# Where the feed-forward weights are split into halves: at each later stage, or once in the cross-attention, kept in memory

## The reference

```python
x = x + xattn(layernorm(x), ctx)   # 16 heads of 64, softmax over 257 keys, w_q, w_k, w_v, w_o, b_o
x = x + attn(layernorm(x))         # causal over the 32 rows, 16 heads of 32, a bias of -log1p(decay * log1p(dist))
x = x + ffn(layernorm(x))
# ffn: h = round8(x @ w1 + b1)           w1 is 512 x 2048
#      h = piecewise linear GELU of h, rounded to multiples of 2**-8
#      out = round8(h @ w2 + b2)         w2 is 2048 x 512
```

## Time and profile before

| | |
|---|---|
| runs | 1636.91, 1637.39, 1634.85 us; median 1636.91 |
| the profiled execution's span, first to last instruction | 1631.5 us (the profile gives no time around it; the median stands 5.4 us above) |
| busy: PE | 1582.6 us, 97% of the span |
| busy: DVE, ACT, POOL | 1229.8 (75%), 1033.8 (63%), 771.8 (47%) |
| DMA | 173.63 MB, mean 106 GB/s |
| granted clock of TensorE, mean | 0.993 of full |

### The profile page before, as it was taken

One profiled execution on the slowest core, in us unless ns is written; L12 is line 12 of the kernel. 1 busy time (PEld: TensorE's weight loads), 2 busy tenths in 40 slices (PEclk: granted clock), 3 DMA queues, 4 the chain that ended last, 5 costly groups with the idle time before them and its releaser, 6 DMA issues. The chain is left out here.

```text
span 1631.5 us, 30117 instructions
## 1 busy us (share of the span) xinstructions
PE 1582.6 (97%) x11126; PEld 1382.6 (85%) x11126; DVE 1229.8 (75%) x2404; ACT 1033.8 (63%) x2050; POOL 771.8 (47%) x722
## 2 busy tenths in 40 slices
PE   7999999999999999999999999999998999999998
PEld 5878899998999999899999778988886777878886
DVE  5548888877887888878887784666666988788886
ACT  3347777777777777777786422445446766666665
POOL 2316546364554546555453241334435545555554
PEclk9999999999999999999999999999998999999999
DMA  7983434444343443534353862011132221010010
GB/s 232 276 244 95 135 91 113 121 112 134 90 123 111 108 134 95 140 95 110 114 144 83 290 220 72 21 60 62 64 111 79 71 71 53 26 52 20 7 52 26
DMA packets 173826, 173.63 MB, mean 106 GB/s; under 512 B 80944, under 2 KB 138352, under 8 KB 173680
## 3 DMA queue, kind: packets, MB, share of 16 engines
q1 hardware_dynamic: 173680, 171.71, 36.2%
HBM read 133.91 MB, written 37.75 MB: 105 GB/s over the span
## 5 line engine op out<-in xcount | busy, mean ns | idle before, releaser
L75 PE MATMUL p_bank_score<-p_ctxt,p_qo 128*128 128x256 f32 x2304 | 304.5, 286 | 1.0 <-ACT p_probs L998 0.6
L75 PEld LDWEIGHTS p_bank_score<-p_ctxt,p_qo 128*128 128x128 f32 x2304 | 288.1, 191 | 6.1 <-issue 2.4
L75 PE MATMUL p_bank_mix<-p_probt,p_ctx 128*128 128x512 f32 x1152 | 292.1, 398 | 0.5
L75 PEld LDWEIGHTS p_bank_mix<-p_probt,p_ctx 128*128 128x128 f32 x1152 | 207.5, 189 | 41.8 <-issue 3.8
L2017 PE MATMUL p_bank_down<-p_w,p_ht 128*128 128x512 f32 x768 | 188.2, 393 | 7.0 <-DVE p_raw L2091 4.9
L1990 POOL TENSOR_TENSOR p_pieces<-p_pieces 128x512 f32<-128x512 f32 x64 | 112.3, 1755 | 159.2 <-ACT p_pieces L2057 159.2
L1201 DVE SCALAR_TENSOR_TENSOR p_qo<-p_bank_mix,p_odd,p_qo 128x512 fp32r<-128x512 f32 x192 | 143.8, 749 | 57.2 <-ACT p_qo L1012 49.5
L704 POOL TENSOR_TENSOR p_ctx<-p_ctx_in,p_ctx 128x768 fp32r<-128x768 f32 x64 | 118.3, 1849 | 131.6 <-ACT p_ctx L987 131.2
L2017 PEld LDWEIGHTS p_bank_down<-p_w,p_ht 128*128 128x128 f32 x768 | 143.8, 188 | 42.1 <-DVE p_raw L2091 6.5
L1012 ACT ACTIVATE p_qo<-p_bank_mix,p_odd 128x512 fp32r<-128x512 f32 x192 | 132.2, 689 | 67.8 <-PE p_bank_mix L75 67.4
L998 ACT ACTIVATE p_probs<-p_bank_score,p_small 128x257 f32<-128x257 f32 x256 | 121.3, 475 | 58.9 <-DVE p_small L1182 54.4
(11 more groups left out here) (276 smaller groups left out, 3631.9 us busy)
## 6 DMA issues: line engine op xcount, KB each, us to landing
p_blocks_in<-in_ctx_dram SPq DMA_DIRECT2D x256, 96.0 KB, 2.4
p_ctx_in<-in_ctx_dram SPq DMA_DIRECT2D x64, 384.0 KB, 3.1
q<-p_ctx SPq DMA_DIRECT2D x64, 256.0 KB, 3.6
p_odd_in<-in_ctx_dram SPq DMA_DIRECT2D x64, 192.0 KB, 3.5
p_x<-in_x_dram SPq DMA_DIRECT2D x32, 256.0 KB, 4.2
p_quad<-q SPq DMA_DIRECT2D x32, 256.0 KB, 3.8
p_probt<-q SPq DMA_DIRECT2D x32, 256.0 KB, 4.1
p_o_in<-o SPq DMA_DIRECT2D x8, 1024.0 KB, 7.1
```

Of the source, the lines that this page charges most:

```text
L75: made = e.matmul(out, lhsT, rhs, start=n == 0, stop=n == last)
```

## The change

All 32 blocks of 128 x 512 of w_1 and w_2 are split within the cross-attention's batches by GpSimd, one block at the end of each of the first six batches of a group (groups 0 to 4; two blocks in group 5). SP loads a block into `w_raw[0]` (before the loads of `blocks_in` in its order), GpSimd casts it into `w_raw[1]` and writes the low half over the block, and SP stores both halves in a new internal tensor `ffn` in the batch after. The next load waits for both stores. In batch 6 of a group SP waits for the stores before it loads the first query tile.

The later stages only load the halves, 512 KB in one DMA a block: the first four blocks of w_1 at the self-attention's start, the other twelve in its steps 12, 13 and 14, those of w_2 in the feed-forward, four at its start and one a unit, each when the load four before it has landed. All splits there, with their buffers, semaphores and waits, are gone. PE waits for the loads in place of the splits. In the feed-forward `rest_of(1)` moves into its place in unit 1 as in every other unit.

The diff, cut to its core (declarations, buffers' names and the removed helper functions of the split are left out):

```diff
             return sum(len(blocks[i][0]) for i in range(k + 1) if buffer(i) == buffer(k))
+        ffn_blocks = [w_1[k * P:(k + 1) * P, c * C:(c + 1) * C] for c in range(F // C) for k in range(KT)]
+        ffn_blocks += [w_2[k * P:(k + 1) * P, :] for k in range(F // P)]
+        PER_GROUP = 6
+
+        def ffn_block_of(b):
+
+            j = b // GB * PER_GROUP + b % GB
+            return [j] if b % GB < PER_GROUP and j < len(ffn_blocks) else []
+
         def later(g):
...
                         "(u p) r -> p u r", p=P)).then_inc(q_got[t % NQB], DMA)
+
+            def load_ffn_block(j):
+                if j % PER_GROUP == 0:
+                    e.wait_ge(queried, UNITS * NT * (j // PER_GROUP + 1))
+                else:
+                    e.wait_ge(ffn_out, 2 * DMA * j)
+                e.dma_start(w_raw[0][:], ffn_blocks[j]).then_inc(ffn_in, DMA)
+
+            def store_ffn_block(j):
+                e.wait_ge(ffn_hi, j + 1)
+                e.dma_start(ffn_dram[j, HI], w_raw[1][:]).then_inc(ffn_out, DMA)
+                e.wait_ge(ffn_lo, j + 1)
+                e.dma_start(ffn_dram[j, LO], w_raw[0][:]).then_inc(ffn_out, DMA)
             def store_values(g, t):
...
                 for b in range(g * GB, (g + 1) * GB if g < NG else 0):
+                    for j in ffn_block_of(b - 1) if b % GB > 0 else ():
+                        store_ffn_block(j)
                     if b + 2 < B:
                         load_context(b + 2)
+                    for j in ffn_block_of(b):
+                        load_ffn_block(j)
+                    if b + 2 < B:
                         if b % GB > 0:
                             load_blocks(b + 2)
                         load_odd(b + 2)
                     if b % GB == GB - 2 and g + 1 < NG:
+                        e.wait_ge(ffn_out, 2 * DMA * min((g + 1) * PER_GROUP, len(ffn_blocks)))
                         load_queries(g + 1, 0)
...
                                 ALU.mult, ALU.mult).then_inc(normal, 1)
+
+            def split_ffn_block(j):
+                e.wait_ge(ffn_in, DMA * (j + 1))
+                e.tensor_copy(w_raw[1][:].bitcast(F32R), w_raw[0][:]).then_inc(ffn_hi, 1)
+                e.wait_ge(ffn_hi, j + 1)
+                e.tensor_tensor(w_raw[0][:].bitcast(F32R), w_raw[0][:], w_raw[1][:], ALU.subtract).then_inc(ffn_lo, 1)
             make_identity(e, ident, ident_ready)
...
                     scale(b, tile)
+                for j in ffn_block_of(b):
+                    split_ffn_block(j)
                 if b % GB == GB - 1 and b + 2 < B:
...
                 load_y(i)
+            for k in range(KT):
+                e.dma_start(f32(after.w1[:, :, k, :]), ffn_dram[k].rearrange("s p c -> p s c")).then_inc(after.w_in, DMA)
             for t in range(NT):
                 if t + 7 < NT + after.early:
                     load_x(t + 7)
-                if t + 2 in WEIGHTS:
-                    k = t + 2 - WEIGHTS[0]
-                    if k == 0:
-                        e.wait_ge(made, 7)
-                    else:
-                        e.wait_ge(after.w_lo, k)
-                    e.dma_start(w_raw[:], w_1[k * P:(k + 1) * P, 0:C]).then_inc(after.w_in, DMA)
-                for k in LATE_IN.get(t, ()):
-                    if k == 0:
-                        e.wait_ge(scored, NB * (NT - 2))
-                    if k >= 8:
-                        e.wait_ge(late_odd if k % 2 else late_even, (k - 8) // 2 + 1)
-                    e.dma_start(late_raw[k % 8], late_block(k)[1]).then_inc(late_in[k % 8], DMA)
+                if t in LATE_IN:
+                    c = LATE_IN[t]
+                    if c == 1:
+                        e.wait_ge(valued, NT)
+                        e.wait_ge(keyed, NT)
+                    for k in range(KT):
+                        e.dma_start(f32(wattn[:, :, k, (c - 1) * C:c * C]), ffn_dram[c * KT + k].rearrange(
+                            "s p c -> p s c")).then_inc(after.late_in[c - 1], DMA)
                 e.wait_ge(added, t + 1)
...
                                     ALU.mult).then_inc(normal, 1)
-                for k in late_blocks(LATE_ODD, t, 0):
-                    low_late(k)
                 if t == NT - 2:
                     low_mix(t - 1)
                 if t < NT:
                     e.wait_ge(p_hi, t + 1)
                     e.tensor_tensor(pt[t % 2][:, LO], flat[t % 2][:], f32(pt[t % 2][:, HI]),
                                     ALU.subtract).then_inc(p_lo, 1)
-                if t in WEIGHTS:
-                    k = t - WEIGHTS[0]
-                    e.wait_ge(after.w_hi, k + 1)
-                    e.tensor_tensor(after.w1[:, LO, k, :], w_raw[:], f32(after.w1[:, HI, k, :]),
-                                    ALU.subtract).then_inc(after.w_lo, 1)
                 if t and t != NT - 2:
                     low_mix(t - 1)
-                for k in late_blocks(LATE_ODD, t, 1):
-                    low_late(k)
         def tensor(e):
...
                     high_rows(t + 4)
-                if t in WEIGHTS:
-                    k = t - WEIGHTS[0]
-                    e.wait_ge(after.w_in, DMA * (k + 1))
-                    e.activation(after.w1[:, HI, k, :], w_raw[:], ACT.Copy).then_inc(after.w_hi, 1)
                 if t and t != NT - 2:
                     high_mix(t - 1)
-                for k in late_blocks(LATE_HI, t, 1):
-                    high_late(k)
         def vector(e):
...
                     e.transpose(flat[t % 2][:].rearrange("p h m q -> p (h m) q"), by_head).then_inc(flipped, 1)
-                for k in late_blocks(LATE_EVEN, t, 0):
-                    low_late(k)
                 if t != NT - 2:
                     rows_and_sums(t)
-                for k in late_blocks(LATE_EVEN, t, 1):
-                    low_late(k)
         nc.clear_and_free_semaphores(ended)
...
             def load_block(k):
-                if k >= 2:
-                    e.wait_ge(w_lo, k - 1)
-                e.dma_start(raw[k % 2][:], blocks[k][0]).then_inc(raw_in[k % 2], DMA)
+                if k >= WIDE:
+                    e.wait_ge(w_in[k % WIDE], DMA * (k // WIDE))
+                e.dma_start(f32(w2[:, :, k, :]), ffn_dram[F // C * KT + k].rearrange("s p c -> p s c")).then_inc(
+                    w_in[k % WIDE], DMA)
             def load_x(n):
...
                     at += 1
-                if n == 0:
-                    load_block(0)
-                if n + 1 < KF:
-                    load_block(n + 1)
+                for k in range(WIDE) if n == 0 else (n + WIDE - 1,) if n + WIDE - 1 < KF else ():
+                    load_block(k)
                 if n == 2:
...
                     e.wait_ge(norm.lo, NR * (g + 1))
+                if n == 0:
+                    e.wait_ge(ahead.w_in, KT * DMA)
+                if g == 0 and f > 0 and f % KT == 0:
+                    e.wait_ge(ahead.late_in[f // KT - 1], KT * DMA)
                 if n >= 3:
...
                 if g == 0:
-                    e.wait_ge(w_lo, f + 1)
+                    e.wait_ge(w_in[f % WIDE], DMA * (f // WIDE + 1))
                 e.wait_ge(h_lo, n + 1)
...
                     e.activation(w[:], a[:], ACT.Relu, bias=last[:], scale=-1.0).then_inc(left, 1)
-                    if n == 0:
-                        high_block(0)
                     e.wait_ge(snapped, n + 1)
                     e.activation(g0[:], v[:], ACT.Gelu, bias=base[:]).then_inc(gelu0, 1)
                     e.activation(a[:], v[:], ACT.Gelu, bias=quarter[:]).then_inc(gelu1, 1)
-                    if 0 < n < KF:
-                        high_block(n)
                 if 1 <= n <= NT:
...
                     e.wait_ge(y_done, i - 1)
-                else:
-                    e.wait_ge(w_lo, len(blocks))
                 if i == 0:
                     e.wait_ge(b2_in, DMA)
-                e.tensor_tensor(raw[i % 2][:], b_down[i % NR], b2[:], ALU.add).then_inc(y_cut, 1)
+                e.tensor_tensor(sums[i % 2][:], b_down[i % NR], b2[:], ALU.add).then_inc(y_cut, 1)
             def output(i):
                 e.wait_ge(y_round, i + 1)
                 x_is_in(e, "y", i)
-                e.scalar_tensor_tensor(out=x_of("y", i), in0=raw[i % 2][:], scalar=MAGIC, in1=x_of("y", i),
+                e.scalar_tensor_tensor(out=x_of("y", i), in0=sums[i % 2][:], scalar=MAGIC, in1=x_of("y", i),
                                        op0=ALU.subtract, op1=ALU.add).then_inc(y_done, 1)
...
                     w, v = w_[n % SETS], v_[n % SETS]
-                    if 0 < n <= KF:
-                        low_block(n - 1)
                     e.wait_ge(left, n + 1)
                     e.tensor_scalar(v[:], w[:], SNAP - STEP / 2, None, ALU.add).then_inc(snapped, 1)
-                    if n != 1:
-                        rest_of(n)
+                    rest_of(n)
                 if 0 <= n - 1 < NT:
```

(36 more changed lines are left out.)

36 lines of the change are left out of this document (6 added, 30 removed).

## The result

The changed kernel takes 1640.65 us (median of 12 runs, 1637.86 to 1643.83), the kernel before 1637.41 beside it (12 runs, 1634.50 to 1642.02): ratio 1.0024, 95% interval [1.0016, 1.0032]. Run once more for the experiments it gave 1640.57 against 1637.49, ratio 1.0016 [1.0008, 1.0025]. So it is slower by 3.1 to 3.2 us, little, but neither interval holds 1. The forecast was 1638.3 and "same". By its own cut, "slower" from 1640.2 on, this is just slower, to which it gave 0.29 and not the 0.44 of "same".

The account below looks back on a forecast made before the run. PE, busy 97% of the span, was taken as the bound; -0.2 (self-attention) - 8.5 (feed-forward) + 9.1 + 1.0 (cross-attention) = +1.4 us on the 1631.5 span, plus 5.4, gave 1638.3, range 1630.5 to 1645.5.

Parts of the forecast that it names:

- Cross-attention, first batches: Cross-attention, first batch of groups 0 to 5: late load plus split makes PE lose 1.5 us each, +9.1 in all.
- B: Cross-attention group starts are cheap: first load lands after 2.6 us, loss 6 x 0.7, total 1632.4; chance 0.30.
- Second batches: Cross-attention, second batch of a group: loads of `blocks_in` stand behind the block's waiting load, +1.0 us in all.
- Steady batches: Cross-attention, 26 of 32 blocks: the split fits GpSimd's idle 2.77 us, 0 per batch, bounds 0 and +0.5.
- rival C: Cross-attention: GpSimd or SP bounds every batch, splits end late through store and load landings; +13, 1651 us; chance 0.16.
- Feed-forward: Feed-forward stage: w_2 arrives split, group 0 loses its splits and PE's waits for them; -8.5 us, bounds -5.5 and -9.8.
- first down-product: Feed-forward, group 0: its wait of 0.79 us shrinks by 0.5, bounds 0 and -0.8.
- Over the boundary: Feed-forward, change from group 0 to 1: output-sum waits and slower products go, -4.5 us, bounds -3 and -5.
- with group 1's boundary as the model: Feed-forward: without splits the first boundary costs what the change from group 1 to 2 does, saving 3.7 and 0.9 us.
- Self-attention's end: End of self-attention: late w_1 subtracts on DVE before the last add go, -0.2 us, bounds 0 and -1.5.
- Rival D: Feed-forward gains only half, DVE's first-boundary backlog coming from tile scaling: -4.2 in place of -8.5, 1642.6 us; chance 0.08.
- left as it stood: Whole kernel: the 5.4 us by which the median stands above the profiled span are added unchanged.

Follow-up runs that it names:

- The two runs above: Changed kernel with block loads issued behind those of `blocks_in`: 1694.96 us; version with the first batch free, each GpSimd cast made four times: 1658.82 us.
- the cost run: Kernel before, plus the loads, splits and stores of all 32 blocks in the cross-attention, later stages not using them: 1645.81 us, ratio 1.0053.

## Why the prediction came out as it did

*Cross-attention, first batches: right in mechanism and count.* Six stalls, in the second batch of groups 0 to 5, none in groups 6 and 7, and no clock lost by them: over the batches the granted clock is 1.00 in both profiles of the changed kernel (longest stall 1.4 us). In the run with the loads behind those of `blocks_in`, six of the seven stalls of 1.9 us and more did cost it. Each of the changed kernel's costs 1.1 to 1.7 us with the 0.2 that follows, 8.4 in all (forecast 1.5 each, 9.1). The load took 3.56 us to GpSimd's start where 3.4 was read from the earlier trace rows. The page of the Trainium skill "DMA: Bandwidth & Descriptors", section "Anatomy of one DMA", would give 2.6 by its fit for the software path; the median over the 32 loads is 3.5, so this trace does not agree for this queue. Nor did it come to B.
The forecast placed the load behind the context's, as it was, and took that for given. It did not say that this place made most of the lateness: put ahead, the same load went out 4.3 us earlier against the context's, and the six stalls were gone.
GpSimd and DVE did not lengthen each other's work: over the whole span the means are 749, 677 and 480 ns (`p_qo` and `p_probt` on DVE, the scaling on GpSimd) against 749, 676 and 481 before.

*Second batches: named, and too small.* Forecast +1.0, measured 2.2 us in the changed kernel, above the 0.2 per group; PE's loss shows in the third batches of groups 0 and 1. In group 1 DVE waits 1.64 for `blocks_in` there and GpSimd 2.52 for the second block. No run took the one away without the other: the one meant to made every split late. So which of them makes PE late stays open; with none of the blocks' work on GpSimd (the transfers alone) the third batches of groups 4 and 5 still lose 0.5 each.

*Steady batches: nothing, as forecast.* The room was narrower than it looked. The forecast set rival C's point at 7.4 us for a store's and a load's landing. The two runs above show that other delays bring it about, in a loop through the context's load. And C's argument against itself, 2 to 4 us at most for a transfer of 256 KB, was too kind: in before's own profile four such loads (`p_late_k`) took a median of 5.1, and in the run with the early load one took 6.1.

*Feed-forward: sum near, terms off.* Forecast -8.5. Two profiles that never left the higher clock in this stage allow the comparison without the clock: the cost run, which has before's feed-forward, and the changed kernel. Up-products around the first boundary, the cost run:

```profile
1371.56 2.88 PE L75 MATMUL p_bank_up<-p_zt,p_wattn 128*128 128x512 f32 x12
1381.37 2.89 PE L75 MATMUL p_bank_up<-p_zt,p_wattn 128*128 128x512 f32 x12
1386.82 2.88 PE L75 MATMUL p_bank_up<-p_zt,p_wattn 128*128 128x512 f32 x12
```

The changed kernel:

```profile
1366.76 2.89 PE L75 MATMUL p_bank_up<-p_zt,p_wattn 128*128 128x512 f32 x12
...
1373.13 0.97 PE L1995 MATMUL p_bank_down<-p_w,p_ht 128*128 128x512 f32 x3 [2.10 <-DVE p_sum L2054]
...
1375.33 0.85 PE L75 MATMUL p_bank_up<-p_zt,p_wattn 128*128 128x512 f32 x3
```

From the stage's first up-product (1263.95 and 1264.91) to up-product 20, the last one ahead of the boundary's waits, it is 107.6 against 101.9: -5.8, where -4.0 was forecast. By product it goes 1.5 at the first down-product, then 2.2, 0.8, 0.8 and 0.5. The 1.5 is beyond the term's bound of 0.8, since PE at full clock comes there sooner and waits 1.28 in the cost run, where before's execution waited 0.79. Over the boundary it is 9.81 against 8.57: -1.2, where -4.5 was forecast. The sum is **-7.0**. The step of this term that failed is "with group 1's boundary as the model". The wait of 2.1 us for the output sums is not DVE's backlog from the splits, since it stands at 2.10 with the splits gone; only the 1.04 before it was theirs. The model was flattered by the clock too: from up-product 36 to 37 it is 8.1 us in both profiles that kept theirs, and 6.6 in before's, whose PE came late and waited only 0.43:

```profile
1459.54 0.97 PE L2017 MATMUL p_bank_down<-p_w,p_ht 128*128 128x512 f32 x3 [0.43 <-DVE p_raw L2091]
```

And the slow products after the first boundary in the earlier trace rows were the clock, which fell there in before's execution and not in the cost run's. The bounds of this sum, -5.5 and -9.8, are not those of its terms, which add up to -6.5 and -9.3; the measured -7.0 lies within both.
The profile's own -8.1 holds 1.1 us more from the stage's start, where before's execution lost clock and the changed kernel's did not.

*Self-attention's end: -0.2 forecast.* The stage takes 256.8 (before's) to 257.8 in all profiles; nothing to be seen.

*The sum.* With the measured sizes, 8.4 + 2.2 - 7.0 = +3.6, against +3.2 by the medians; forecast +1.4. Rival D, a gain smaller by 4.3 us, had the right doubt and three times the size. That before's median stood 3.5 us above its one profiled execution, apart from the 2 around the span, was left as it stood. This came out right, without a reason: no profile of an execution near that median was taken, and where those 3.5 us lie is not known. The terms were off by 2.2 us together, all to the same side: the batches cost 0.5 more than forecast, the feed-forward gave 1.5 less, and the 0.2 of the self-attention can't be seen.

## What to carry to other kernels

A block of work moved into another engine's idle slot needs two things at once there, the engine's time and its data, and one of them alone may be hidden where both are not: find where the data's load stands in the issuing queue, and what that queue waits for ahead of it. Where the work stands ahead of something that the next load waits for, add up the whole loop, through the issuing queue as well, and hold it against the period, not the work against the gap. And put such work where the pipeline is steady: leaving the first of a group's eight batches free turned +3.2 us into -7.9.

## What the runs showed of the hardware

The granted clock after a pause is not settled by the pause. All twelve profiles have the same 2.1 to 2.2 us without a product ahead of the feed-forward's first. In the 12 us that follow six stay at 1.00 and six fall, before's to 0.86; the version with the first batch free is one of these, the changed kernel not. First the changed kernel, then that version:

```profile
1264.90:1276.90 12.00, 11.99 (x53) 9.89 (x54) 6.71 (x16) 8.38 (x12) 3.14 (x5) 1.00 0.94 284
```

```profile
1253.00:1265.00 12.00, 11.99 (x46) 9.70 (x47) 5.50 (x14) 7.82 (x12) 2.52 (x4) 0.86 0.94 296
```

That costs 1.1 to 1.5 us. A fall at the first boundary costs another 1.6 at most and is given back at the second: PE comes later there and waits only the 0.43 shown above for before's, where the changed kernel waits 1.54 first:

```profile
1465.17 0.96 PE L1995 MATMUL p_bank_down<-p_w,p_ht 128*128 128x512 f32 x3 [1.54 <-DVE p_sum L2054]
1466.56 0.96 PE L1995 MATMUL p_bank_down<-p_w,p_ht 128*128 128x512 f32 x3 [0.43 <-DVE p_sum L2054]
```

In the cross-attention's batches the picture is the same: a stall of 1.88 us at 282.74 in the run with the late loads left the clock at 1.00, one of 1.88 at 623 in the same execution was followed by a window of 10 us at 0.83. Of the changed kernel's stalls, 1.4 us at most, none was. What decides whether the clock falls was not tried and stays open.
